# A decoder layer on one core: attention blocks, state sums, row products and first gates moved in their queues

## The reference, cut to what matters

```
x = layernorm(x + attention(x))            # 16 heads, 4 kv heads, over the 4 "positions" s of a token column
x = layernorm(x + ssm(ctx, z=x))           # selective scan: 512 channels, 16 states, 512 steps
x = layernorm(x + ffn(x))                  # silu(x Wg) * (x Wu), then Wd; weights are lut[idx], 16 values

# the scan, per channel e and state n
state = state * exp(delta * A) + (delta * u) * B ;  y += state * C
y = (y + D * u) * silu(z)
```

## Time and profile before

| | |
|---|---|
| median of 3 runs | 993.14 us (989.9 to 993.56) |
| the profiled execution | 993.16 us, its span 991.4 us |
| PE matmul busy | 867.5 us (88%) |
| DVE busy | 759.4 us (77%) |
| ACT busy | 672.3 us (68%) |
| POOL busy | 497.1 us (50%) |
| mean granted TensorE clock | 0.909 of full speed |

### The profile page before, as it was taken

How to read it: one execution, slowest core, us unless ns; L and a number is a source line. 1 busy time by engine, 2 the same in 40 slices (tenths; PEclk the granted TensorE clock), 3 DMA queues, 4 the chain that set the end, 5 groups by cost and what they waited for, 6 DMA issues and landing times.

```text
span 991.4 us, 11868 instructions
## 1 busy us (share of the span) xinstructions
PE 867.5 (88%) x3824; PEld 625.8 (63%) x3824; DVE 759.4 (77%) x1053; ACT 672.3 (68%) x994; POOL 497.1 (50%) x458
## 2 busy tenths in 40 slices
PE   7879798797888787786979888899999999899997
PEld 3447554476445564456545466787777778688885
DVE  3697899877998879986779566888888888355542
ACT  4598985789956899668696465677777776242321
POOL 0069867799767998669899631122111211001000
PEclk9789877989779897787989889999999999999999
DMA  7156989689985799968999222111111110223211
GB/s 247 51 162 166 224 162 210 139 219 250 211 212 118 203 240 214 221 125 205 208 278 280 88 96 85 43 50 57 42 42 42 48 58 21 74 85 107 85 64 53
DMA packets 49907, 135.98 MB, mean 137 GB/s; under 512 B 5364, under 2 KB 13684, under 8 KB 41156
## 3 DMA queue, kind: packets, MB, share of 16 engines
q0 software_dynamic: 8064, 58.72, 30.7%
q1 hardware_dynamic: 40432, 76.44, 23.0%
q10 hardware_dynamic: 1364, 0.25, 0.2%
HBM read 57.93 MB, written 78.51 MB: 138 GB/s over the span
## 4 chain that ended last, share of the span: by engine, by line
PE 27%; issue 23%; DVE 20%; ACT 18%; POOL 5%; DMA 5%; DVEq 1%; ACTq 0%; POOLq 0%; SPq 0%
PE banks L596 6%; PE banks L707 5%; ACT decay L880 5%; ACT scaled L869 5%; DVE state L1170 5%; PE banks L731 4%; DVE leaf L1198 3%; POOL state L1419 3%; PE banks L634 3%; PE banks L538 3%; DVE w_gu L1198 2%; ACT leaf L988 2%; DMA hT<-y_scratch 2%; DVE conv_in L1081 2%; DMA y_scratch<-state 1%
## 5 line engine op out<-in xcount | busy, mean ns | idle before, releaser
L1419 POOL TENSOR_TENSOR state<-state,crep 128x512 f32<-128x512 f32 x256 | 353.0, 1639 | 70.7 <-DVE state L1170 68.9
L1170 DVE TENSOR_TENSOR_SCAN state<-decay,banks 128x512 f32<-128x512 f32 x256 | 295.9, 1203 | 60.6 <-PE banks L634 45.4
L707 PE MATMUL banks<-x2T,wgu 128*128 128x512 f32 x1056 | 246.5, 393 | 4.9 <-DVE hT L1249 3.9
L634 PE MATMUL banks<-ident,scaled 128*128 128x128 f32 x1024 | 173.3, 311 | 72.3 <-DVE state L1170 53.4
L707 PEld LDWEIGHTS banks<-x2T,wgu 128*128 128x128 f32 x1056 | 197.9, 189 | 52.5 <-DVE hT L1249 11.1
L634 PEld LDWEIGHTS banks<-ident,scaled 128*128 128x128 f32 x1024 | 135.2, 160 | 145.7 <-DVE state L1170 64.9
L880 ACT ACTIVATE decay<-delta,negA 128x512 f32<-128x512 f32 x256 | 170.1, 724 | 77.4 <-DVE state L1170 77.0
L869 ACT ACTIVATE scaled<-duT,BT 128x512 f32<-128x512 f32 x256 | 163.8, 721 | 0.0
L988 ACT ACTIVATE leaf<-idx_sb,table,table_gap 128x1024 f32<-128x1024 uint8 (+1 forms) x132 | 129.5, 1023 | 6.7 <-DVE w_down L1198 3.2
L1198 DVE COPY_PREDICATED leaf<-idx_sb,leaf 128x1024 f32<-128x1024 uint8 (+1 forms) x88 | 94.1, 1070 | 6.4 <-issue 5.5
L1509 POOL TENSOR_TENSOR pool_wait_here<-minus_half 128x1 f32<-128x1 f32 x22 | 4.3, 194 | 179.7 <-DVE w_gu L1198 115.3
(11 more groups left out here) (138 smaller groups left out, 1136.3 us busy)
## 6 DMA issues: line engine op xcount, KB each, us to landing
y_scratch<-state POOLq DMA_DIRECT2D x52, 1024.0 KB, 8.7
crep<-c_scratch SPq DMA_DIRECT2D x64, 256.0 KB, 5.4
idx_sb<-in_idx SPq DMA_DIRECT2D x11, 512.0 KB, 3.5
xT_sb<-in_xT SPq DMA_DIRECT2D x16, 256.0 KB, 4.7
y_scratch<-u SPq DMA_DIRECT2D x4, 1024.0 KB, 6.3
y_scratch<-state SPq DMA_DIRECT2D x4, 1024.0 KB, 6.3
leaf<-x_scratch SPq DMA_DIRECT2D x16, 256.0 KB, 2.7
out<-leaf SPq DMA_DIRECT2D x16, 256.0 KB, 2.0
```

The lines of the kernel that those rows point to most:

```text
L634: last = nc.tensor.transpose(banks[:, k % NB, lc * LQ:(lc + 1) * LQ], scaled[:, g % SR, lc, et * P:(et + 1) * P], ident[:])
L707: last = mm(banks[:, 2 * tb + w, :], wgu[par][:, w, ws, t * P:(t + 1) * P], x2T[:, tb, xs, t, :], start=t == 0 and n == 0, stop=t == HT - ...
L1170: V.tensor_tensor_scan(state[:, g % GR, et, :], decay[:, k % DR_RING, :], banks[:, k % NB, :], 0.0, ALU.mult, ALU.add).then_inc(scan_ready, 1)
L1419: G.tensor_tensor(state[:, g % GR, et, :], state[:, g % GR, et, :], crep[:, g % CR, :], ALU.mult)\
```

## The change

It moves instructions within the queues of PE, ACT, DVE and POOL; none is added or left out.

- PE transposes the attention of position 2 at (3, 2) instead of (4, 1) in blocks 0 to 2, and ACT reads it out in row 3 instead of row 4.
- PE's four kv jobs stand at (4, 3), (5, 1), (5, 3), (6, 2) instead of (4, 2), (4, 3), (6, 0), (6, 1). ACT reads kv 0 and 1 in row 5 instead of 4, kv 3 in row 6 instead of 5, and the attention of position 1 behind kv 2 instead of ahead of it.
- PE's sums of the last 8 rows come 7 units behind its transposes instead of 12; 7 instead of 12 are left after the last.
- POOL's first two powers of the row stage stand ahead of its product of sequence 2 (`gate_row(2)`) instead of behind it.
- `silus(0, 0)` and `silus(0, 1)` on ACT, and `inner(0, 0)` and `inner(0, 1)` on DVE, stand ahead of the first `tile` (on ACT also ahead of `high_part(1, 1)`) instead of inside it.

```diff
+        SUM_LAG = 7
-                   (4, 2): ("kv", 0), (4, 3): ("kv", 1), (6, 0): ("kv", 2), (6, 1): ("kv", 3),
+                   (4, 3): ("kv", 0), (5, 1): ("kv", 1), (5, 3): ("kv", 2), (6, 2): ("kv", 3),
-        ATT_AT = {(3, 0): 3, (3, 1): 0, (4, 1): 2, (6, 0): 1}
+        ATT_AT = {(3, 0): 3, (3, 1): 0, (3, 2): 2, (6, 0): 1}
# PE, the loop over units
-                    if k // ET - 3 >= G0:
-                        state_summed(k // ET - 3, k % ET)
-                for g in range(DS * S - 3, DS * S):
-                    for et in range(ET):
-                        state_summed(g, et)
+                    if k - SUM_LAG >= ET * G0:
+                        state_summed(*divmod(k - SUM_LAG, ET))
+                for k in range(UNITS - SUM_LAG, UNITS):
+                    state_summed(*divmod(k, ET))
# ACT, row n of a block
-                        elif n == (4 if more else 3):
+                        elif n == 3:
                             keep_attT(b, 2)
-                        elif n == (5 if more else 4):
+                        elif n == 4 and not more:
                             keep_attT(b, 1)
                             elif n == 4:
                                 keep_bc(m)
+                            elif n == 5:
                                 keep_kv(c, 0)
                                 keep_kv(c, 1)
-                            elif n == 5:
                                 keep_kv(c, 2)
-                                keep_kv(c, 3)
+                                keep_attT(b, 1)
                                 keep_bt(m)
                             elif n == 6:
+                                keep_kv(c, 3)
                                 keep_uT(m)
# ACT, ahead of high_part(1, 1)
+                silus(0, 0)
+                silus(0, 1)
# DVE, ahead of tile(0)
+                inner(0, 0)
+                inner(0, 1)
# both: inside tile the calls for blocks 0 and 1 only where f is a loop's register
+                    if not isinstance(f, int):
# POOL
                 last_leaf(*FIRST)
+                stage2_rstd(0)
+                stage2_rstd(1)
                 gate_row(2)
-                for k in range(5):
+                for k in range(2, 5):
                     stage2_rstd(k)
```

More of the change, by code:

```diff
@@ L1036, in tile @@
                     leaves("down", f)
-                    silus(f, 0)
+                    if not isinstance(f, int):
+                        silus(f, 0)
                     leaves("gate_up", f + 2, early)
-                    silus(f, 1)
+                    if not isinstance(f, int):
+                        silus(f, 1)
                     leaves("gate_up", f + 2, late)
@@ L1335, in tile @@
                     select("down", f, then=("gate_up", f + 2))
-                    inner(f, 0)
+                    if not isinstance(f, int):
+                        inner(f, 0)
                     select("gate_up", f + 2, range(3), then=("down", f + 1))
-                    inner(f, 1)
+                    if not isinstance(f, int):
+                        inner(f, 1)
                     select("gate_up", f + 2, range(3, 6), then=("down", f + 1))
```

## The result

The kernel after takes 996.04 us (median of 20 runs, 993.57 to 999.69); the kernel before, run beside it, takes 993.15 us (20 runs, 989.26 to 995.51). The ratio is 1.0040 [1.0029, 1.0051], +4.0 us [+2.9, +5.1]. The profiled executions differ by less: the span is 994.1 us, before 991.4, which is +2.7. They are one execution each, so the ratio decides the size, and the trace shows the place.

What follows compares the result with a forecast made beforehand. ACT, closely followed by the landings, paces the crowded scan stretch; DMAs, DVE's small operations and selects bound later stages. 0 + 0 + 4.2 - 0.6 = +3.6 us on 993.16 gives 996.8 us; 8-of-10 range 989.8 to 1000.6.

Steps and rivals of the forecast that it cites:

- Powers ahead of the product: Row stage: POOL's product, now behind the second power, holds DVE's select and delays residual(4): +4.2 us, bounds 0 and +4.5.
- a loss in either order: Row stage: had DVE's select gone first, the later product would make x2T_hi(0) 3.1 us late instead.
- First silus and inners: Start of the ffn: moved into idle time, taking one 0.60 us step from the selects' chain: -0.6 us, bounds 0 and -2.5.
- Attention and kv: Scan blocks 0 to 2: ACT and landings pace, so moving PE's work gives 0; bounds -0.6 and +3 us.
- Rival B: Scan blocks: PE's crowded stretch is the pacer, thinning it wins 8.5 us, 988.3 us in all; chance 0.13.
- Rival C: Rows 6 to 8: ACT's later kv reads hold PE, 1.5 us a block, 1001.3 us in all; chance 0.17.
- The cover of that 0: Landing in blocks 1 and 2 and DVE's 1.31 us wait in block 0 hide PE's loss, otherwise 0.5 us a block.
- log term: Block 1 softplus: ACT's input taken as ready at 244.88, DVE starting at 245.20, so only 0.32 us could be won.
- Sums: End of the scans: last sum waits for POOL's product, rest sums for a load: cost 0, bounds -0.2 and +0.5 us.
- faster by more than 5 us: Whole kernel: chance 0.11 of a gain beyond what a measurement can tell from no change, called most of half of B.

Runs made afterwards that it cites:

- pow_alone: The kernel before with only the two powers moved ahead of POOL's product of sequence 2: 996.45 us, ratio 1.0038 to the kernel before.
- product_halves: The kernel after with POOL's product of sequence 2 split into two instructions of 128x1024: 996.54 us, ratio 1.0033 to the kernel before.
- pe_twice: The kernel before with PE's attention of position 2 run twice in blocks 0 to 2: 998.53 us, ratio 1.0046 to the kernel before.
- sums_alone: The kernel before with only the sums seven units behind instead of twelve: 992.17 us, ratio 0.9995 to the kernel before.
- undo_pow: The kernel after with the powers behind the product of sequence 2 again: 992.58 us, ratio 1.0004 to the kernel before.
- high_behind: The kernel before with first silus and inners moved and ACT's gate/up high part behind the next down chunk's first four leaves: 986.88 us, ratio 0.9946.

## Why the prediction was right

The forecast of 996.8 us lies 0.8 from the median, and the mechanism of its one large term is the one seen.

- **Powers ahead of the product, +4.2.** Measured +3.8 (pow_alone by time, 3.78 at residual(4)). Step by step: the product was to start at 570.59, it did at 570.48; the select was to wait until 575.13 and end near 576.5, it ended at 576.13. Half of the missing 0.4 is the tail of the select behind the product: it was 1.14 us, where its full 1.36 had been added, although the prediction's own row at 624.58 shows a tail of 0.63 us for a select of 0.77. The other half was won ahead of this edit, as PE's rest sums took 6.05 us instead of 6.22; counted from the first residual the loss is 3.96 us. The Trainium skill (SBUF — State Buffer, section "SBUF: two separate sides") has VectorE and GpSimd exclude each other on a shared port pair for a whole instruction. The trace agrees to within some 0.2 us (the tail of 1.14 against 1.36): 5.33 us beside 4.51, 3.23 beside 2.35, and in product_halves the hold goes both ways, as an exclusive lock would. The prediction's "a loss in either order" was not tried.
- **First silus and inners, -0.6.** -0.75 in the trace and some -0.8 over the nine traces; by the times -2.0 [-3.4, -0.5], an interval that holds the forecast and goes beyond its lower bound of -2.5. PE's wait of 2.54 us went, and stands as 1.75 us at 646.27, two blocks on, as said.
- **Attention and kv, 0.** Right, and the details too: (4, 2) 0.7 us earlier (0.6 forecast), ACT's kv read at 228.16 (228.2), `bt` released at 228.58 (228.6), (6, 2) 0.5 us earlier (0.6), (6, 3) 0.55 us later (0.3 to 0.5), row 7 at its old time to 0.1 us. The block as a whole lay 0.2 us earlier than before (the silu of u at 208.99, before 209.20), so the details hold to some 0.2 us. One missed: the scan at (6, 1) came 1.5 us earlier, not 2.5. Reading ACT's 38.33 of 38.40 us, with the landings, as the bound was the decisive step. Rival B would have had row 7 start 2 us earlier. Rival C's place was right too (scans wait 1.31 and 2.46 us for PE in row 6), but the 0.48 us that row 7 had waited for the landing covered it.
- **The cover of that 0.** The prediction let the landing and DVE's 1.31 us in block 0 hide up to 0.5 us of lateness on PE. That holds for 0.5 us, and pe_twice shows that it doesn't for 2.7 us, of which over half came through, most in block 0: there DVE already waited for ACT, so its 1.31 us cover a late scan, but not a late ACT.
- **A reading that was wrong.** The prediction took the log term to be ready at 244.88, the end of both its instructions, and so saw 0.32 us to be won in block 1. The softplus needs only the first, which ended at 243.78 + 0.61 = 244.39; block 0 shows the same, with ACT's pair from 117.38 and DVE's start at 118.02. The slack was 0.81 us, and the best bound for two such blocks some -1.6, not -0.6. The forecast of 0 didn't hang on it.
- **Sums, 0.** sums_alone is 0 within 1.5 us. PE's last sum still waits for POOL's product and the rest sums for the load, as said. That the rest sums start at 553.70, before 553.63, is luck, since this start scatters by several us.
- **The size.** 3.47 - 0.75 = 2.7 us in the two traces is just below the interval [2.9, 5.1] of the times. Of this, the 0.17 us of the rest sums and the 0.31 between residual(4) and gate and up differ by over 1 us among kernels with the same code there. The two parts that other traces repeat give 3.96 - 0.75 = +3.2 us, within the interval and below the +3.6 of the sum. The ratio says 4.0 us and the bare medians 2.9, so that 996.8 lies within 0.8 us of the median is in part luck.
- **The chances.** The 0.11 for "faster by more than 5 us" is called most of half of rival B, but half of its 0.13 is 0.07.

## What to carry to other kernels

The length of an instruction in the profile can contain a wait that no semaphore marks: where the same form takes 5.33 us at one place and 1.36 at another, look for what the neighbouring engine has under way. Here the long GpSimd product was free beside VectorE's additions from PSUM and cost 3.8 us beside its select. Slack has a direction: a stretch from which nothing is won by thinning it can still cost over half of what is added to it (1.5 of 2.7 us). In a loop that several engines hand around, follow the wait with a name (the select behind ACT's leaves) and move what stands ahead of the awaited work, since taking the visible stretch out of one instruction may only move it to the next.

## What the runs showed of the hardware

Small operations are held too. POOL and then DVE of undo_pow, where the same power stands once beside a select and once alone:

```profile
570.18 1.77 POOL L1509 TENSOR_TENSOR rstd<-vareps,minus_half 128x2 f32<-128x2 f32 x1 [2.47 <-DVE vareps L1235]
575.35 0.70 POOL L1509 TENSOR_TENSOR rstd<-vareps,minus_half 128x2 f32<-128x2 f32 x1 [3.40 <-DVE vareps L1235]
...
570.05 1.38 DVE L1203 COPY_PREDICATED w_gu<-idx_sb,leaf 128x1024 f32<-128x1024 uint8 x1
```

The power of two columns takes 1.77 us instead of 0.70, as it starts 0.13 us behind the select. In high_behind (POOL, then DVE) an addition that reads PSUM lies wholly within a product and keeps the 0.69 us that it has elsewhere:

```profile
552.79 4.53 POOL L1504 TENSOR_TENSOR rows_in<-rows_in,gate_in 128x2048 f32<-128x2048 f32 x1
...
555.12 0.69 DVE L1219 TENSOR_TENSOR hT<-banks,hT 128x512 f32<-128x512 f32 x1 [0.94 <-PE banks L649]
```

The addition and the select differ in where their operands lie and in the operation as well; which of the two decides isn't separated here.

And holds cascade: in product_halves the select that was held by the first half ends at 570.78 + 3.23 = 574.01, and the second half, issued at 572.75, does its 2.35 us behind that (574.01 + 2.35 = 576.36, and it ends at 576.26).
